# Down projection of a feed-forward stage by seven half-size products per block instead of eight

## The reference, cut to what matters

```python
x = act_qdq(x)                                   # round to 16 bits by the largest absolute value of the whole tensor
up = act_qdq(x @ lpbq_dequant(w_up).T)           # 512 -> 1536
gate = act_qdq(x @ lpbq_dequant(w_gate).T)
sig = fixed_qdq_u16(sigmoid(gate))
gate = act_qdq(gate * sig)
o = act_qdq(gate * up)                           # round(gate * up / scale) * scale
return o @ lpbq_dequant(w_down).T                # 1536 -> 512, the down projection
```

## Time and profile before

| | us |
|---|---|
| median of 3 runs (4806.02 to 4810.66) | 4807.38 |
| the profiled execution: its own time | 4805.85 |
| its span, first to last instruction | 4803.8 |
| mean granted TensorE clock, share of full speed | 0.939 |

### The profile page before, as it was taken

How to read it: one execution, slowest core, us unless ns; L and a number is a source line. 1 busy time by engine, 2 the same in 40 slices (tenths; PEclk the granted TensorE clock), 3 DMA queues, 4 the chain that set the end, 5 groups by cost and what they waited for, 6 DMA issues and landing times. The chain is left out here.

```text
span 4803.8 us, 50266 instructions
## 1 busy us (share of the span) xinstructions
PE 4028.3 (84%) x15992; PEld 2289.8 (48%) x15992; DVE 3419.7 (71%) x3827; ACT 2409.1 (50%) x4734; POOL 2588.8 (54%) x1527
## 2 busy tenths in 40 slices
PE   7898977799999459989937888888888879978987
PEld 6766875444444124433314555555555543445554
DVE  5654438522377556548878999999999978955677
ACT  1211115322345631127857888888888865423333
POOL 4545965000033011109868999999999976622221
PEclk9999997699999779999969999999999999989999
DMA  3332235232278765435543242242251226710100
GB/s 110 107 103 72 72 112 165 88 105 103 112 275 304 291 262 198 171 108 190 187 180 130 70 140 92 74 162 70 69 180 58 67 86 257 267 60 18 35 27 36
DMA packets 363929, 625.71 MB, mean 130 GB/s; under 512 B 67238, under 2 KB 152647, under 8 KB 351634
## 3 DMA queue, kind: packets, MB, share of 16 engines
q1 hardware_dynamic: 325506, 578.92, 34.5%
q10 hardware_dynamic: 38160, 43.56, 2.5%
HBM read 394.24 MB, written 228.15 MB: 130 GB/s over the span
## 5 line engine op out<-in xcount | busy, mean ns | idle before, releaser
L2315 POOL TENSOR_TENSOR sc_X<-sc_Bm,sc_w 128x1024 f32<-128x1024 f32 x512 | 1192.4, 2364 | 88.5 <-DVE sc_H L2494 64.4
L1375 PE MATMUL ff_ps<-ffn_R,hand_w 128*128 128x512 f32 x1536 | 660.6, 592 | 0.7 <-ACT ffn_R L1414 0.7
L2337 ACT ACTIVATE sc_A<-sc_dt,keep_A 128x1024 f32<-128x1024 f32 x512 | 581.7, 1136 | 83.7 <-DVE sc_Z L2499 63.1
L2367 ACT ACTIVATE sc_hT<-sc_tp,sc_ct 128x128 f32<-128x128 f32 x2048 | 584.6, 375 | 72.5 <-PE sc_tp L2421 69.7
L2421 PE MATMUL sc_tp<-sc_idn,sc_H 128*128 128x128 f32 x2048 | 316.6, 277 | 223.2 <-issue 144.3
L2442 PE MATMUL sc_yp<-sc_Z,sc_idn 128*128 128x512 f32 x1024 | 486.3, 597 | 9.9 <-ACT sc_yo L2373 9.6
L1375 PEld LDWEIGHTS ff_ps<-ffn_R,hand_w 128*128 128x128 f32 x1536 | 291.2, 190 | 364.6 <-issue 362.8
L2421 PEld LDWEIGHTS sc_tp<-sc_idn,sc_H 128*128 128x128 f32 x2048 | 233.6, 141 | 438.6 <-issue 250.7
L2494 DVE TENSOR_TENSOR_SCAN sc_H<-sc_A,sc_X 128x1024 f32<-128x1024 f32 x160 | 358.9, 2273 | 23.9 <-ACT sc_A L2337 12.7
L2494 DVE TENSOR_TENSOR_SCAN sc_H<-sc_A,sc_hc,sc_X 128x1024 f32<-128x1024 f32 x160 | 368.4, 2336 | 2.2 <-ACT sc_A L2337 2.2
L75 POOL TENSOR_TENSOR gp_pbd<-gp_r,ssm_msk 128x512 f32<-128x512 f32 x144 | 182.2, 1265 | 221.2 <-DVE gp_r L478 221.2
(11 more groups left out here) (423 smaller groups left out, 8058.5 us busy)
## 6 DMA issues: line engine op xcount, KB each, us to landing
sc_Bm<-d_xd SPq DMA_DIRECT2D x64, 512.0 KB, 7.4
ffn_gate_d<-ff_o SPq DMA_DIRECT2D x96, 256.0 KB, 2.3
ffn_up_d<-ff_o SPq DMA_DIRECT2D x96, 256.0 KB, 6.3
ffn_g_d<-ff_z SPq DMA_DIRECT2D x24, 1024.0 KB, 6.8
ffn_R<-ffn_up_d SPq DMA_DIRECT2D x22, 1024.0 KB, 13.3
ffn_R<-ffn_g_d SPq DMA_DIRECT2D x19, 1024.0 KB, 10.7
hand_x<-d_x SPq DMA_DIRECT2D x16, 1024.0 KB, 7.3
ff_g<-ffn_gate_d SPq DMA_DIRECT2D x16, 1024.0 KB, 6.3
```

Of the source, the lines that this page charges most:

```text
L1375: last = nc.tensor.matmul(ps[:, 2 + t % 6], w[:, k, h * P:(h + 1) * P], xt[:, n, k], start=(k == 0), stop=(k == KD - 1))
L2315: nc.gpsimd.tensor_tensor(X[:, k % RX], Bm[:, n], w[:, j % 2], ALU.mult).then_inc(db, 1)
L2337: nc.scalar.activation(A[:, k % 2], dt[:, j % 2], ACT.Exp, scale=keepA[:, n:n + 1]).then_inc(ex, 1)
L2367: nc.scalar.activation(hT[:, turned(k) % 2, q], tp[:, b * P:(b + 1) * P], ACT.Copy, scale=ct[:, i % 2, q, n:n + 1]).then_inc(tc, 1)
```

## The change

Blocks 1 to 7 are multiplied by Strassen's scheme (in Winograd's form). Block rows are split into halves i = 0, 1 (the 512 tokens are seen as 2 w x 2 i x 128), the 12 slices of k into j = 0, 1 (6 each), and the 512 output columns into two halves. Instead of 8 products of such half-size parts there are 7. Each product is 2 w * 6 k = 12 matmuls of 128 x 128 against 128 x 256, so a block has 84 (168 instructions). In return:

- GpSimd makes four sums of the rounded rows per block (`row_sums`, each 128 x 1536), written over `gd[n % 2]`, and once four sums of the weights (`down_sums`, 128 x 1536), written over `z`. It does `round_up(n+1)` ahead of `row_sums(n)`.
- VectorE adds the parts onto the residual rows in 8 pieces of 128 x 512 (`add_rows`), spread between its other operations, where it had 4 in `finish`. `product` is cut in two.
- The residual rows get a second buffer (`g[:, 0]`). The load of `up` for block n is issued once block n-2 has made its third product and its sums; the load of `gate` when all products of block n-2 are done, since the sums lie in that buffer. ScalarE takes MAGIC off block n+2 after it has issued the store of block n.

The order on TensorE for a block (in brackets the bank): A11 B11 (0), A12 B21 (1), A22 T4 (2), then, once VectorE has taken bank 0, S2 T2 onto it, S1 T1 (3), then S3 T3 onto bank 0, once VectorE has taken it again, and S4 B22 onto bank 3. A11 is half i = 0 of the rows with k half 0, and so on. Block 0 stays as it was.

```diff
+        rows = [x[:], g[:, 0].rearrange("p (a d) -> p a d", a=4)]
+        osum = [[r[:, HB_ * TB + 4 * j * 3 * P:HB_ * TB + 4 * (j + 1) * 3 * P].rearrange("p (k w t) -> p k w t", k=HK, w=2) for j in range(4)] for r in (R1, R0)]
...
@@ sync @@
-            for n in range(1, NB):
-                if n == 1:
-                    sp.wait_ge(cmx, 1 + NT_)
-                if n > 1:
-                    sp.wait_ge(dmm, 1 + (n - 1) * NU)
-                load_block(n)
-                if n > 1:
-                    sp.wait_ge(yok, 1 + (n - 1) * NU)
-                    sp.dma_start(x[:], xr[n - 1]).then_inc(rin, 16)
...
+            for n in range(3, NB):
+                sp.wait_ge(dr_, 1 + n - 2)
+                sp.wait_ge(os4, 1 + 4 * (n - 2))
+                load_block_up(n)
+                sp.wait_ge(dq_, 1 + 2 * (n - 2))
+                load_block_g2(n)
+                sp.wait_ge(yok, 1 + (n - 1) * NU)
+                load_rows(n)
@@ gpsimd @@
+            def row_sums(n):
...
+                pool.wait_ge(r2, 1 + NPC + n)
+                nc.gpsimd.tensor_tensor(s1, a21, a22, ALU.add).then_inc(os4, 1)
+                pool.wait_ge(os4, 1 + c + 1)
+                nc.gpsimd.tensor_tensor(s2_, s1, a11, ALU.subtract).then_inc(os4, 1)
+                nc.gpsimd.tensor_tensor(s3, a11, a21, ALU.subtract).then_inc(os4, 1)
+                pool.wait_ge(os4, 1 + c + 2)
+                nc.gpsimd.tensor_tensor(s4, a12, s2_, ALU.subtract).then_inc(os4, 1)
...
-            for n in range(1, NB):
-                round_up(n)
+            round_up(1)
+            down_sums()
+            row_sums(1)
+            round_up(2)
+            for n in range(2, NB):
+                if n + 1 < NB:
+                    round_up(n + 1)
+                row_sums(n)
@@ tensor @@
+            def down(n, b, a, m, onto, done):
+                for w in range(2):
+                    for k in range(HK):
+                        last = nc.tensor.matmul(ps[:, n % 2 * NU + b, w * HD_:(w + 1) * HD_], a[:, k, w], m[:, k],
+                                                start=(w == 0 and k == 0 and not onto), stop=(w == 1 and k == HK - 1), skip_group_check=onto)
+                last.then_inc(done, 1)
...
             for n in range(1, NB):
                 pe.wait_ge(r2, 1 + NPC + n)
-                for u in range(NU):
-                    if n > 1:
-                        pe.wait_ge(res, 1 + (n - 2) * NU + u + 1)
-                    for k in range(HB_):
-                        last = nc.tensor.matmul(ps[:, v * NU + u], zd[v][:, k, u * P:(u + 1) * P], downT[:, k], start=(k == 0), stop=(k == HB_ - 1))
-                    last.then_inc(dmm, 1)
...
+                down(n, 0, rows_of(n, 0, 0), down_of(0, 0), False, dp_)
+                down(n, 1, rows_of(n, 0, 1), down_of(1, 0), False, ds_)
+                down(n, 2, rows_of(n, 1, 1), down_sum(3), False, dr_)
+                added(n, 1)
+                down(n, 0, row_sum(n, 1), down_sum(1), True, dp_)
+                down(n, 3, row_sum(n, 0), down_sum(0), False, dq_)
+                added(n, 4)
+                down(n, 0, row_sum(n, 2), down_sum(2), True, dp_)
+                added(n, 5)
+                down(n, 3, row_sum(n, 3), down_of(1, 1), True, dq_)
@@ vector @@
+            def add_rows(n, q):
...
+                nc.vector.scalar_tensor_tensor(out=v, in0=ps[:, n % 2 * NU + b].rearrange("p (w c) -> p w c", w=2), scalar=scale, in1=v,
+                                               op0=ALU.mult, op1=ALU.add).then_inc(xa, 1)
...
-            for n in range(NB):
-                if n + 1 < NB:
-                    round_g2_block(n + 1)
-                    product(n + 1)
-                    round_o(n + 1)
-                finish(n)
+            finish_first()
+            for n in range(1, NB):
+                more = n + 1 < NB
+                if n > 1:
+                    finish(n - 1)
+                dve.wait_ge(rin[n % 2], 1 + (n // 2 + 1) * 16)
+                add_rows(n, 0)
+                if more:
+                    round_g2_block(n + 1)
+                add_rows(n, 1)
+                add_rows(n, 2)
+                if more:
+                    product_part(n + 1, 0, 2)
+                add_rows(n, 3)
+                if more:
+                    product_part(n + 1, 1, 2)
+                add_rows(n, 4)
+                if more:
+                    scale_o(n + 1)
+                add_rows(n, 5)
+                add_rows(n, 6)
+                if more:
+                    round_o(n + 1)
+            finish(NB - 1)
```

More of the change, by code:

```diff
@@ L1307, in _, with load_block_g2, load_block_up, load_rows @@
                 sp.wait_ge(st[r], 1 + 2 * NG // NO * 16)
[L1309 to L1312, removed]
+            def load_block_g2(n):
+                sp.dma_start(gd[n % 2], g2_b[:, :, n * TB:(n + 1) * TB]).then_inc(dgi[n % 2], 16)
+            def load_block_up(n):
+                sp.dma_start(zd[n % 2], up_b[:, :, n * TB:(n + 1) * TB]).then_inc(dzi[n % 2], 16)
+            def load_rows(n):
+                sp.dma_start(rows[n % 2], xr[n]).then_inc(rin[n % 2], 16)
             for m in range(6, NT_):
@@ L1484, in _ @@
                 act.dma_start(yr[n], y[:]).then_inc(yst, 16)
+                if n + 2 < NB:
+                    less_magic_block(n + 2)
             act.wait_ge(yst, 1 + NB * 16)
@@ L1571, in round_g2_block, with product_part @@
                 nc.vector.tensor_scalar(gd[v], gd[v], s2.mul, MAGIC, ALU.mult, ALU.add).then_inc(d1, 1)
-            def product(n, p=None):
-                v, o_ = n % 2, zd[n % 2] if p is None else zd[0][:, p * HP:(p + 1) * HP]
-                gq = gd[v] if p is None else gd[0][:, p * HP:(p + 1) * HP]
+            def product_part(n, p, parts):
+                k = slice(p * HB_ // parts, (p + 1) * HB_ // parts)
+                o_, gq = zd[n % 2][:, k], gd[n % 2][:, k]
                 dve.wait_ge(d2, 1 + n + 1)
@@ L1578, in product, with round_o_first, scale_o, round_o @@
                 nc.vector.scalar_tensor_tensor(out=o_, in0=o_, scalar=MAGIC, in1=gq, op0=ALU.subtract, op1=ALU.mult).then_inc(dpr, 1)
[L1580 to L1583, removed]
+            def round_o_first(p):
+                o_ = zd[0][:, p * HP:(p + 1) * HP]
+                dve.wait_ge(dpr, 1 + p + 1)
                 nc.vector.tensor_scalar(o_, o_, os_.mul, MAGIC, ALU.mult, ALU.add).then_inc(r1, 1)
-                dve.wait_ge(r1, 1 + k)
+                dve.wait_ge(r1, 1 + p + 1)
                 nc.vector.tensor_scalar(o_, o_, MAGIC, None, ALU.subtract).then_inc(r2, 1)
[L1588 to L1596, removed]
+            def scale_o(n):
+                dve.wait_ge(dpr, 1 + NPC + 2 * n)
+                nc.vector.tensor_scalar(zd[n % 2], zd[n % 2], os_.mul, MAGIC, ALU.mult, ALU.add).then_inc(r1, 1)
+            def round_o(n):
+                dve.wait_ge(r1, 1 + NPC + n)
+                nc.vector.tensor_scalar(zd[n % 2], zd[n % 2], MAGIC, None, ALU.subtract).then_inc(r2, 1)
+            def norm(n):
                 nn.mean_rstd(nc, dve, n)
@@ L1599, in finish, with finish_first @@
                     dve.wait_ge(yst, 1 + n * 16)
-                    nn.apply(nc, y[:, u], x[:, u], u).then_inc(yok, 1)
+                    nn.apply(nc, y[:, u], rows[n % 2][:, u], u).then_inc(yok, 1)
+            def finish_first():
+                dve.wait_ge(rin[0], 17)
+                for u in range(NU):
+                    dve.wait_ge(dmm, 1 + u + 1)
+                    nc.vector.scalar_tensor_tensor(out=x[:, u], in0=ps[:, u], scalar=os_.s, in1=x[:, u], op0=ALU.mult, op1=ALU.add).then_inc(res, 1)
+                for u in range(NU):
+                    dve.wait_ge(res, 1 + u + 1)
+                    nc.vector.bn_stats(nn.st[:, u, 0], x[:, u]).then_inc(nn.stats, 1)
+                norm(0)
+            def add_rows(n, q):
+                i, j, b, scale, sem, count = (
+                    (0, 0, 0, os_.s, dp_, 3 * n - 2), (0, 0, 1, os_.s, ds_, n), (1, 0, 2, nos[:], dr_, n), (0, 1, 0, os_.s, dp_, 3 * n - 1),
+                    (1, 1, 3, os_.s, dq_, 2 * n - 1), (1, 0, 0, os_.s, dp_, 3 * n), (1, 1, 0, os_.s, dp_, 3 * n), (0, 1, 3, os_.s, dq_, 2 * n))[q]
+                v = rows[n % 2].rearrange("p (w i) (j c) -> p w i j c", i=2, j=2)[:, :, i, j]
+                dve.wait_ge(sem, 1 + count)
+                dve.wait_ge(xa, 1 + 8 * (n - 1) + (0, 1, 0, 0, 0, 3, 5, 4)[q])
+                nc.vector.scalar_tensor_tensor(out=v, in0=ps[:, n % 2 * NU + b].rearrange("p (w c) -> p w c", w=2), scalar=scale, in1=v,
+                                               op0=ALU.mult, op1=ALU.add).then_inc(xa, 1)
+            def finish(n):
+                add_rows(n, 7)
+                for u in range(NU):
+                    dve.wait_ge(xa, 1 + 8 * n)
+                    nc.vector.bn_stats(nn.st[:, u, 0], rows[n % 2][:, u]).then_inc(nn.stats, 1)
+                norm(n)
             for m in range(NT_):
```

76 lines of the change are left out of this document (64 added, 12 removed).

## The result

The changed kernel takes 4821.23 us (median of 11 runs, 4817.71 to 4825.31), the kernel before, run beside it, 4810.66 (11 runs, 4804.19 to 4814.82): a ratio of 1.0025, 95% interval 1.0016 to 1.0034. It is slower by some 12 us, where the forecast said 18 on its 4807.4.

What follows compares the result with a forecast made beforehand. TensorE bounds the kernel before; with the change, port turns between GpSimd and VectorE make rounds 45.5 us. Start 1.5, five rounds 20.5, block 6 -0.5, block 7 -3.5 sum to +18: 4825 us, range 4790 to 4850.

Steps and rivals of the forecast that it cites:

- TensorE, 36.1 us a block: Down projection: 168 instructions of 256 columns, 0.43 us per pair, make a block cost 36.1 us instead of 41.4.
- Sums, 3.4: GpSimd's four sums per block take 3.4 us each, 13.6 together, by the line through two measured sizes.
- The port: VectorE and GpSimd lock the shared memory port for whole instructions; 37.7 us per block can't overlap.
- Rival 1: Sums at their upper bound of 3.8 us and worse turns: time 4834 to 4846; chance 0.13.
- Rival 2: GpSimd's long instructions let VectorE in between: rounds of 36.6 us, time 4778; chance 0.20.
- The first part of the round, 15.2 us: Start of each round: four sums and `apply` take turns and end at 15.2 us.
- Five rounds at +4.1 each, 20.5: Rounds 1 to 5 take 45.5 us instead of 41.4 each, adding 20.5 us.
- Start, +1.5: Sums of the weights, in turn with the rounding of block 1, make block 1 start 1 to 2 us late.
- Block 7, -3.5: Last block has nothing to round for: 36.1 + 0.6 and up to 2 us half clock, so -4 to -3.
- Half clock, 2 us, absorbed: TensorE after idling runs at half clock, some 2 us per block, taken up by the wait to 28.7 us.
- What costs nothing: Second buffers and smaller edits (earlier row loads, ScalarE's order) cost nothing, covered by the 15.9 us before `round_g2_block`.
- Rival 3: `round_up` hides, or additions and turns fall better: rounds of 40.9 us, 23 us off, time 4802; chance 0.14.

Runs made afterwards that it cites:

- experiment 1: Changed kernel with each of the four sums per block cut to one number per partition; 4805.13 us, ratio 0.9997 to the kernel before.
- experiment 3: Changed kernel with `round_up` of blocks 2 to 7 on ScalarE instead of GpSimd; 4804.23 us, ratio 0.9995 to the kernel before.
- experiment 2: Changed kernel with the four `apply` operations per block on ScalarE, sums at full length; 4800.86 us, ratio 0.9991 to the kernel before.
- experiment 6: Changed kernel with `apply` moved behind the next block's first scaling and one addition; 4804.20 us, ratio 0.9998 to the kernel before.
- experiment 4: Changed kernel with `apply` and `round_up` (blocks 2 to 7) both on ScalarE; 4789.98 us, ratio 0.9964 to the kernel before.
- 7: Kernel of experiment 4 with `round_up(2)` back on GpSimd; 4787.63 us, ratio 0.9964 to the kernel before.
- experiment 5: Kernel before with four unread sums a block added on GpSimd, eight products kept; 4806.32 us, ratio 1.0003 to the kernel before.

## Why the prediction was right

The sign and the mechanism came out as forecast; the size was 12 us instead of 18. That the time itself is so near (4821 for 4825) is in part luck: the kernel before, run beside the changed one, was itself 3.3 us slower than the 4807.4 on which the forecast stands. The phase itself is 11.2 us longer in the profiled executions (333.4 from first to last matmul before, 344.6 after). By its steps:

- **TensorE, 36.1 us a block.** Right: in block 7 the last of the products starts 20.76 us after the fourth one before it (2060.99 to 2081.75), 5.19 each, 36.3 a block; the block as a whole is 36.6.
- **Sums, 3.4.** Right: 3.44 where VectorE is quiet, 3.6 in turn with `apply`. Rival 1 (3.8) fell.
- **The port.** Right. The rule that the port is held for the whole instruction, cited from the Trainium skill (SBUF — State Buffer, section "SBUF: two separate sides"), holds for long instructions too in this trace: a scaling takes 8.12 us when `round_up` has begun, and `round_up` takes 8.12 when a scaling has (8.57 in experiment 1). Rival 2, by which VectorE gets in between, fell.
- **The first part of the round, 15.2 us.** In the round shown the sums end at 14.1 and `apply` at 14.9. Scaling done at 19.3: 18.9. Products done at 32.0: 31.6. `round_up` done at 37.3: 37.1. End at 45.5: 45.0. The load of `up` came otherwise than forecast, and it didn't matter here. It is issued at 17.5 instead of 15.2, since it also waits for the third product, and that is later at the lower clock; it takes 14.3 us where 15 were put in (13.7 to 15.3 in the others), and lands at 31.7 instead of 30, still just ahead of VectorE's scaling at 32.2.
- **Five rounds at +4.1 each, 20.5.** Too high, and the term that was mis-sized: they average 44.7, together 16.3 above five times 41.4, or 17.1 above what the same five rounds take in the kernel before (41.2 each). Three of them, 44.7 to 45.4, go as forecast and are 0.5 us shorter in the mean. The two of 44.1 go the other way round at the last collision. Timeline of the changed kernel, GpSimd and VectorE, in the round that starts at 1832.34:

```profile
1864.54 3.41 DVE L1679 TENSOR_SCALAR ffn_R<-ffn_R,hand_scx 128x6144 f32<-128x6144 f32 x1
1865.09 8.12 POOL L1367 TENSOR_SCALAR hand_w<-hand_w,hand_scx 128x6144 f32<-128x6144 f32 x1 [18.62 <-DMA hand_w<-ffn_up_d]
...
1869.18 7.23 DVE L1683 TENSOR_SCALAR ffn_R<-ffn_R 128x6144 f32<-128x6144 f32 x1
```

  The load lands 32.8 us into the round instead of 31.7 (32.5 in the other one), after the scaling has begun. Now `round_up` has to wait, its own 5.4 us begin under the two additions, and the subtraction pays 3.9 us where the scaling paid 4.7. The prediction took the order of the two as fixed; half a microsecond decides it. Why the load lands a microsecond later in these two stays open. The later issue alone isn't the reason: in experiment 3, with TensorE at full rate, a load issued at 15.8 lands at 31.7 too.
- **Start, +1.5.** Measured 0.6. **Block 6, -0.5:** -1.6. **Block 7, -3.5:** -4.9. (Both against the kernel before's own 41.8 and 41.5; the four parts, 0.6 + 17.1 - 1.6 - 4.9, are the phase's 11.2.) That the start's small delay comes from the sums of the weights is argued from the order of the instructions; no run leaves them out. The last came out lower because TensorE had idled only 1.21 us before it and ran at full rate; the half-clock time put in for it did not come.
- **Half clock, 2 us, absorbed.** Right for TensorE itself: the first 48 instructions take 12.1 to 13.6 instead of 10.6, and the later wait is 0.65 instead of the forecast 2.5. Where it is no longer absorbed, in experiments 1 and 2, it shows in the round: of the rounds of blocks 2 to 5 in these two runs, those that begin with 10.63 us take 38.8 and 38.9 us, those with 12.31 take 40.4 to 40.5, and the one with 13.29 takes 41.5.
- **What costs nothing.** The `gate` load was covered by the turns; experiment 2 shows what lies under the cover: scaling then starts at 8.7 us, set by that load.
- **Rival 3** (`round_up` hides) did not happen, but experiments 3 and 6 bear out its round: 40.9 was forecast, they have 38.5 to 41.4, most of them 40 to 41, and the kernel is level with the one before. Its 23 us were too many, 13 to 14 by the ratios, since the changed kernel's own rounds are shorter than 45.5 and the round of block 1 gains next to nothing.

Removing either collision gives some 4.3 us a round in blocks 2 to 5: `apply` (experiments 1 and 2), `round_up` (3). The round of block 1 gains nothing by it: 46.3 to 47.1 us in these three, 45.4 in the changed kernel. Removing both brings blocks 2 to 7 to 37.3 in the mean (4), near TensorE's 36.3, and the phase to 312.5 us from its first to its last matmul, 21 less than before. That is what of the scheme's 36 us (7 blocks by 5.1) can be had this way: of the other 15, 8 lie in the round of block 1, which the transfers set (7), 6 in the six rounds behind it. The prediction had said of block 1, under rival 2, that it gains nothing without the port's turns, because `up(2)` is loaded behind `gate(2)`: so it is, but for the 1 to 2 us by which 44.4 and 43.6 are below 45.4.

Open stays a smaller thing. The parts of the kernel outside this phase are the same instructions, but in the profiled executions the changed kernel spends some 8 us more on them (the span is 19.4 longer, the phase 11.2), experiment 4 some 4 more. The runs of one kernel spread over 7 to 14 us, and the medians of the changed kernel lie 11 apart from those before, so most of this may be the spread of single executions. By the ratios the changed kernel is 12 us slower, which leaves next to nothing outside the phase. But experiments 1, 2, 3 and 6 have phases 5 to 9 us shorter than the kernel before's and are by the ratios only 1 to 4 us faster; the intervals are some 4 us wide to either side. No run shows whether a part of it belongs to the change.

## What to carry to other kernels

An idle engine is not a free resource if it shares a memory port with a busy one: add up who holds the port and, above all, look for short instructions of one engine between long ones of the other, since each short one waits for a whole long one. What it costs depends on the place: on the chain to the next block every us counts, in a wait it is free (experiment 5), so an order can be worth as much as the removal of one collision (experiment 6). And when a bound is taken away from one engine, ask which engine was hiding under it; here giving work to ScalarE, whose four normalised rows took 2.94 us beside the sums and 2.93 without them, was what made the scheme pay.

## What the runs showed of the hardware beyond expectation

- **Turns go both ways and alternate.** With both engines asking, each instruction lets one of the other pass: in the two sums beside `apply` they take 3.6 and the four `apply` 10.66 (0.5 and three times some 3.4). While weights are summed and block 1 is rounded, every instruction of both is twice as long: sums 6.60 and 6.62, scaling 6.51.
- **The lower clock after a wait of 2.3 us comes in some rounds and not in others.** In experiments 1 and 2 the 48 instructions behind an idle time of 2.28 us took 12.31 us in some rounds and 10.63 in others, in experiment 2 once 10.63 even behind 3.53; behind 1.21 it was 10.63 in all runs. In the changed kernel two stretches at the start of a round show it (the last but two columns are the clock): after 5.7 and 5.9 us without a matmul it is at or near half, 1.2 of 2.4 GHz, then full.

```profile
1921.00:1925.00 4.00, 3.81 (x10) 3.13 (x11) 3.65 (x10) 0.14 (x1) 3.70 (x2) 0.56 1.04 391
1966.00:1970.00 4.00, 3.84 (x9) 3.13 (x10) 3.62 (x10) 0.17 (x1) 3.73 (x2) 0.50 1.01 378
1925.00:1929.00 4.00, 4.00 (x21) 3.51 (x20) 3.77 (x3) 0.16 (x1) 4.00 (x2) 1.00 0.07 26
```

What tells the rounds at 2.28 us apart stays open, and with it some 1.6 us per round of experiments 1 and 2.
